# A four-block graph network on one core: SyncE's list of transfers written anew, and ScalarE's wait for its receivers' one-hots cut in two

## The reference

```
h = max(layernorm(x), 0); x = x + relu(mean_dst(h[src]) @ W_l.T + b_l + h @ W_r.T)              # L0
h = max(layernorm(x), 0); h1 = relu(mean_dst(h[src]) @ W1l + b1 + h @ W1r)                      # L1A
                          x = x + mean_dst(h1[src]) @ W2l + b2 + h1 @ W2r                       # L1B
h = max(layernorm(x), 0); x = x + LN(h + relu(h @ Ws.T + bs + mean_src(h[dst] @ Wn.T + bn)))    # L2
h = max(layernorm(x), 0); x = x + gcn(relu(gcn(h, W1, b1)), W2, b2)                             # L3A, L3B
```

## Time and profile before

| | before |
|---|---|
| median of 3 runs | 694.64 us (693.9 to 694.92) |
| the profiled execution | 693.28 us, span 691.5 us |
| mean granted clock of TensorE | 0.97 |
| TensorE busy | 631.2 us, 91% of the span |
| VectorE / ScalarE / GpSimd busy | 401.4 / 303.9 / 85.3 us |
| chain that ended last | TensorE 76%, DMA 8%, VectorE 6%, SyncE's queue 4%, issue 3% |

### The profile page before, as it was taken

The page is one execution under the profiler, slowest core; times in us unless marked ns, Lnnn a source line. Parts: engine busy times, 40 slices in busy tenths (PEclk is TensorE's granted clock), DMA queues, the critical chain, the costliest instruction groups (busy, mean ns, idle before and its releaser), DMA issues.

```text
span 691.5 us, 11104 instructions
## 1 busy us (share of the span) xinstructions
PE 631.2 (91%) x3047; PEld 512.7 (74%) x3048; DVE 401.4 (58%) x875; ACT 303.9 (44%) x628; POOL 85.3 (12%) x135
## 2 busy tenths in 40 slices
PE   6889999999108999999999896999999999999997
PEld 4556677778106888888888775888888898889886
DVE  6989989858108653333355476865599942350312
ACT  5968766642004345432123223222458864464320
POOL 4433432100000000000000000000135243000000
PEclk9999999999658999999999998999999999999999
DMA  6200425215785342124244424544210000000102
GB/s 226 84 1 21 55 41 76 40 62 95 142 196 139 68 95 64 61 68 120 56 95 97 100 78 102 138 95 101 63 61 2 0 2 1 0 1 1 46 16 90
DMA packets 151842, 48.38 MB, mean 70 GB/s; under 512 B 133500, under 2 KB 137396, under 8 KB 151800
## 3 DMA queue, kind: packets, MB, share of 16 engines
q1 hardware_dynamic: 150520, 45.34, 28.2%
q10 hardware_dynamic: 1280, 2.56, 1.0%
HBM read 30.44 MB, written 17.44 MB: 69 GB/s over the span
## 4 chain that ended last, share of the span: by engine, by line
PE 76%; DMA 8%; DVE 6%; SPq 4%; issue 3%; ACT 1%; POOL 0%; DVEq 0%; ACTq 0%; POOLq 0%
PE ps L1667 30%; PE ps L1760 18%; PE ps L1797 12%; PE ps L1823 8%; PE ps L1646 7%; DMA rows<-squares 2%; SPq L467 2%; SPq L449 2%; DMA wstage<-in_L_gnn_W1r 2%; DMA count_rows<-count_squares 2%; DMA swap<-count 1%; DVE src_hot L1159 1%; DVE stats L1131 1%; DVE own L1380 1%; DMA wstage<-rows 1%
## 5 line engine op out<-in xcount | busy, mean ns | idle before, releaser
L1760 PE MATMUL ps<-p_hi,cstage 128*128 128x512 f32 x400 | 158.8, 397 | 43.0 <-DVE own L1380 37.6
L1760 PE MATMUL ps<-p_lo,cstage 128*128 128x512 f32 x400 | 157.8, 394 | 0.0
L1667 PE MATMUL ps<-w_hi,hT_hi 128*128 128x512 f32 x320 | 126.2, 395 | 0.6 <-issue 0.4
L1667 PE MATMUL ps<-w_hi,hT_lo 128*128 128x512 f32 x320 | 124.6, 390 | 0.0
L1667 PE MATMUL ps<-w_lo,hT_hi 128*128 128x512 f32 x320 | 124.6, 389 | 0.0
L1760 PEld LDWEIGHTS ps<-p_hi,cstage 128*128 128x128 f32 x400 | 76.6, 191 | 61.7 <-DVE own L1380 39.5
L1760 PEld LDWEIGHTS ps<-p_lo,cstage 128*128 128x128 f32 x400 | 76.5, 191 | 15.9
L1646 PE MATMUL ps<-src_hot,dst_hot 128*128 128x320 bf16 x420 | 65.5, 300 | 7.4 <-DVE src_hot L1159 4.3
L1159 DVE TENSOR_SCALAR src_hot<-iota,nodeT 128x640 bf16<-128x640 f16 x210 | 68.6, 384 | 5.5 <-PE ps L1646 3.5
L1667 PEld LDWEIGHTS ps<-w_hi,hT_hi 128*128 128x128 f32 x320 | 60.1, 188 | 13.4 <-issue 0.9
L1667 PEld LDWEIGHTS ps<-w_hi,hT_lo 128*128 128x128 f32 x320 | 60.1, 188 | 12.6
(11 more groups left out here) (156 smaller groups left out, 963.3 us busy)
## 6 DMA issues: line engine op xcount, KB each, us to landing
rows<-squares SPq DMA_DIRECT2D x38, 256.0 KB, 2.4
zT<-rows SPq DMA_DIRECT2D x120, 64.0 KB, 2.5
count_rows<-count_squares SPq DMA_DIRECT2D x10, 320.0 KB, 2.2
countT<-count_rows SPq DMA_DIRECT2D x40, 80.0 KB, 3.2
x<-in_x ACTq DMA_DIRECT2D x1, 2304.0 KB
out_x<-x SPq DMA_DIRECT2D x9, 256.0 KB
wstage<-rows SPq DMA_DIRECT2D x32, 64.0 KB, 2.4
wstage<-in_L_gnn_W SPq DMA_DIRECT2D x2, 1024.0 KB, 5.6
```

The lines of the kernel that those rows point to most:

```text
L1667: last = nc.tensor.matmul(ps[:, bank, :], a[:, r, k, :], w[:, slot, k, :], start=n == 0, stop=n == len(pairs) - 1)
L1760: last = nc.tensor.matmul(ps[:, AGG + r, :], cstage[:, part, k, :], p_[:, k, :], start=n == 1, stop=n == 2 * len(parts) * NT)
```

## The change

1. SyncE's list. Parking and turning become steps of their own ("tp" and "tr" for counts, "park" and "turn" for the rest), so other steps stand between them. W1r is loaded behind the parking of count block 6, ahead of four turns of count blocks, bias row and swap, instead of behind them all. The swap moves from L0's aggregation to the products of L1B, behind the parking of tile 9. The turns of L2's weights are interleaved with those of L1B's tiles.
2. VectorE makes squares earlier (`SQUARED_AT`): all ten of L1B in L1A's aggregation, W_neigh's four pieces in the first four products of L1B, W_self's four at i = 1 and 2 of L1B's aggregation (were 2 and 3), six of L1A's and L2's tiles during the aggregation ahead (were four).
3. Turned weight pieces count on semaphores of their own (`weight_in`), turned counts on two (`cT_loaded[k]`), and a count turn from block 2 on waits until the turn two blocks back has landed.
4. ScalarE, in `receivers`, waits for the first half of its ring ahead of the first `apart` and for the second half ahead of the third, instead of for the whole ring ahead of the first.

Nothing is computed otherwise. A part on GpSimd's general path, which doesn't run here, is left out below.

```diff
+    SQUARED_AT = {L0: [(), (), (0,), (1,), (), (), (2,), (3,), (4,), (5,)], L1A: [(i,) for i in range(NT)],
+                  L1B: [(), (), (), (0,), (1,), (2,), (3,), (4,), (5,), ()]}
...
-            turns = {s: [("h", (s, i)) for i in range(NT)] for s in (L1A, L1B, L2)}
-            order += [("t", b) for b in range(BY_COUNTING)] + loads[:1] + [("t", b) for b in range(BY_COUNTING, NT)]
-            order += [("v", rows[2]), ("s", None)] + loads[1:2]
-            order += turns[L1A][:2] + loads[2:3] + [("v", rows[5])] + turns[L1A][2:]
-            order += loads[3:4] + turns[L1B][:2] + [("v", rows[6])] + loads[4:5] + turns[L1B][2:]
-            turned_weights = [("h", (None, j)) for j in range(2 * KF)]
-            order += turned_weights[:KF] + loads[5:6] + turned_weights[KF:] + turns[L2][:2] + loads[6:7] + turns[L2][2:]
+            def tail(s):
+                return [step for i in range(6, NT) for step in turns(s, i - 2) + parks(s, i)] + turns(s, 8, 9)
+
+            W = None
+            order += [step for b in range(BY_COUNTING) for step in (("tp", b), ("tr", b))] + loads[:1]
+            order += [("tp", 6)] + loads[1:2] + [("tr", 6), ("tp", 7), ("tr", 7), ("tp", 8)] + parks(L1A, 0)
+            order += [("tr", 8), ("tp", 9)] + parks(L1A, 1) + [("tr", 9)] + turns(L1A, 0, 1) + [("v", rows[2])]
+            order += loads[2:3] + [("v", rows[5])]
+            order += parks(L1A, 2) + turns(L1A, 2) + parks(L1A, 3) + turns(L1A, 3) + parks(L1A, 4, 5) + tail(L1A)
+            order += loads[3:4] + parks(L1B, 0, 1) + turns(L1B, 0, 1) + [("v", rows[6])] + parks(L1B, 2, 3, 4, 5)
+            order += loads[4:5] + turns(L1B, 2) + parks(L1B, 6) + turns(L1B, 3) + parks(L1B, 7, 8, 9) + [("s", None)]
+            order += turns(L1B, 4) + parks(W, 0) + turns(L1B, 5) + parks(W, 1) + turns(W, 0) + turns(L1B, 6) + parks(W, 2)
+            order += turns(W, 1) + turns(L1B, 7) + parks(W, 3) + turns(W, 2) + turns(L1B, 8) + turns(W, 3) + turns(L1B, 9)
+            order += loads[5:6] + parks(W, 4, 5) + turns(W, 4) + parks(W, 6) + turns(W, 5) + parks(W, 7) + turns(W, 6)
+            order += parks(L2, 0) + turns(W, 7) + parks(L2, 1) + turns(L2, 0, 1) + parks(L2, 2, 3) + loads[6:7]
+            order += turns(L2, 2) + parks(L2, 4) + turns(L2, 3) + parks(L2, 5) + tail(L2)
...
+                elif kind == "tr":
+
                     sp.wait_ge(counts_parked, 16 * (what + 2))
+                    if what > 1:
+                        sp.wait_ge(cT_loaded[what % 2], 64 * (what // 2))
...
                     if s is not None:
                         sp.wait_ge(lo_done, tile(s, i - 2))
+                    elif i > 1:
+                        wait_turned_weight(sp, i - 2)
...
                     t = tile_at(act, n, offset)
-                    act.wait_ge(first_rows[h], n + RING)
                     for e in range(BY_ACT):
+                        if e % 2 == 0:
+                            act.wait_ge(first_rows[h], n + (1 + e // 2) * RING // 2)
                         nc.scalar.activation(apart[h][:, e:e + 1, :], tab[:, window(b, h), :], ACT.Abs, scale=-1.0,
...
                             lo(s, i + 2, i % 2)
-                        if i < NT - 4:
-                            square(s, i + 4, i % 2)
-                        elif s == L1B:
-                            square_weight(i - (NT - 4))
+                        if i < 4:
+                            if s == L1B:
+                                square_weight(i)
+                            else:
+                                square(s, i + 6, i % 2)
...
-                        if s == L1B and i in (2, 3):
-                            square_weight(KF + 2 * i - 4)
-                            square_weight(KF + 2 * i - 3)
-                        if i in (2 + late, 3 + late):
-                            square(s + 1, i - 2 - late, i % 2)
-                        if i in (6, 7):
-                            square(s + 1, i - 4, i % 2)
+                        if s == L1B and i in (1, 2):
+                            square_weight(KF + 2 * i - 2)
+                            square_weight(KF + 2 * i - 1)
+                        for k in SQUARED_AT[s][i]:
+                            square(s + 1, k, k % 2)
```

More of the change, by code:

```diff
@@ L228, in gnn_kernel @@
     nodes_placed = sem("nodes_placed")
-    counts_ready, counts_out, cT_loaded = sem("counts_ready"), sem("counts_out"), sem("cT_loaded")
+    counts_ready, counts_out, cT_loaded = sem("counts_ready"), sem("counts_out"), [sem(f"cT_loaded{k}") for k in range(2)]
     vec_loaded = [sem(f"vec{k}_loaded") for k in range(5)]
@@ L250, in gnn_kernel @@
     normed, squared = sem("normed"), sem("squared")
-    parked, turned_in = [[sem(f"{what}{r}") for r in range(2)] for what in ("parked", "turned_in")]
+    parked, turned_in, weight_in = [[sem(f"{what}{r}") for r in range(2)] for what in ("parked", "turned_in", "weight_in")]
     counts_squared, counts_parked = sem("counts_squared"), sem("counts_parked")
@@ L286, in gnn_kernel @@
     BY_COUNTING = 6
+    SQUARED_AT = {L0: [(), (), (0,), (1,), (), (), (2,), (3,), (4,), (5,)], L1A: [(i,) for i in range(NT)],
+                  L1B: [(), (), (), (0,), (1,), (2,), (3,), (4,), (5,), ()]}
     def wait_turned_counts(engine, blocks=NT):
-        engine.wait_ge(cT_loaded, 64 * blocks)
+        for k in range(2):
+            if blocks > k:
+                engine.wait_ge(cT_loaded[k], 64 * ((blocks + 1 - k) // 2))
     def squares_of(dram, m):
@@ L298, in wait_parked, with wait_turned, wait_turned_weight @@
         engine.wait_ge(parked[(n - 1) % 2], 8 * (n + 1 - (n - 1) % 2))
-    def wait_turned(engine, n, r):
-        engine.wait_ge(turned_in[r], 32 * (n + 1 - r))
+    def wait_turned(engine, s, i, r):
+        engine.wait_ge(turned_in[r], 32 * (NT * (s - L1A) + i + 2 - r))
+    def wait_turned_weight(engine, j):
+        engine.wait_ge(weight_in[j % 2], 64 * (j // 2 + 1))
     def wait_loaded(engine, n):
@@ L439, in _, with parks, turns @@
-            turned_weights = [("h", (None, j)) for j in range(2 * KF)]
-            order += turned_weights[:KF] + loads[5:6] + turned_weights[KF:] + turns[L2][:2] + loads[6:7] + turns[L2][2:]
+            def parks(s, *tiles):
+                return [("park", (s, i)) for i in tiles]
+            def turns(s, *tiles):
+                return [("turn", (s, i)) for i in tiles]
+            def tail(s):
+                return [step for i in range(6, NT) for step in turns(s, i - 2) + parks(s, i)] + turns(s, 8, 9)
@@ L450, in _ @@
                             "p h (c q) d -> p (h c) (q d)", q=2).rearrange("p c (g i) -> p c g i", i=32),
-                            squares_of(count_rows[what], m)).then_inc(cT_loaded, 16)
-                elif kind == "h":
+                            squares_of(count_rows[what], m)).then_inc(cT_loaded[what % 2], 16)
+                elif kind == "park":
+                    s, i = what
+                    n = nth(s, i) if s is not None else nth_weight(i)
+                    sp.wait_ge(squared, n)
+                    sp.dma_start(rows_dram[n - 1], squares[:, (n - 1) % 2, :]).then_inc(parked[(n - 1) % 2], 16)
+                elif kind == "turn":
                     s, i = what
@@ L456, in _ @@
                     r = (n - 1) % 2
-                    sp.wait_ge(squared, n)
-                    sp.dma_start(rows_dram[n - 1], squares[:, r, :]).then_inc(parked[r], 16)
                     if n == 1:
@@ L467, in _ @@
                         sp.dma_start(to.rearrange("p k (g i) -> p k g i", i=32),
-                                     squares_of(rows_dram[n - 1], m)).then_inc(turned_in[r], 16)
+                                     squares_of(rows_dram[n - 1], m)).then_inc(
+                                         (turned_in if s is not None else weight_in)[r], 16)
                 elif kind == "s":
@@ L631, in _ @@
                     else:
-                        with pool.Fori(0, NT) as i:
+                        if s == L0:
+                            wait_turned_counts(pool, BY_COUNTING)
+                        with pool.Fori(0, BY_COUNTING) as i:
+                            general_columns(i)
+                        for i in range(BY_COUNTING, NT):
+                            if s == L0:
+                                wait_turned_counts(pool, i + 1)
                             general_columns(i)
```

8 lines of the change are left out of this document (3 added, 5 removed).

## The result

| | before | after |
|---|---|---|
| median | 694.43 us (693.9 to 694.92, 4 runs) | 656.77 us (656.55 to 658.13, 4 runs) |
| ratio of the two | | 0.9462, 95% interval 0.9445 to 0.9478 |
| profiled execution | 693.28, span 691.5 | 656.83, span 655.0 |
| mean granted clock | 0.97 | 0.997 |

A forecast was written before the change was run, and what follows sets the result against it. TensorE, busy 631.2 of 691.5 us, was taken as the bound, so only idle time and slow clock could be won. Terms -28.3 + 0.6 - 12.2 = -39.9 took 694.64 to 654.7 us, range 650 to 662.

The forecast's parts named there:

- What can be had back: Two losses of TensorE: L0's aggregation could end 36.1 us earlier undisturbed, and 12.2 us are lost in L1B's aggregation.
- Term 1, the load's data: Count blocks before L0's aggregation: W1r's early load pushes block 6's turn and block 7's parking back 2.8 us.
- Term 2: L0's aggregation: TensorE waits 4.2 us before tile 6, slow clock costs 2.4, and it ends 28.3 us earlier.
- Term 3, L1A: L1A's products and aggregation: nothing lost, 54.4 + 45.3 us, although VectorE comes 7 us late from L0.
- Term 4, the swap: L1B's products: the moved swap delays tile 4's turn, 0.6 us lost; behind it the margin falls to 2 us and holds.
- Rival B: L1B's products: the swap shows, TensorE waits over 5 us and the clock falls, giving 662.4 us; chance 0.14.
- Term 5, L1B's aggregation: L1B's aggregation: L2's weight pieces are turned earlier, so 12.2 us are won.
- Term 6, the ring: Counting: ScalarE waiting by halves of its ring wins at most 3.7 us, loses at most 1.6; taken as 0.
- A: Before L0's aggregation: W1r's early load costs nothing, giving 651.3 us; chance 0.16.
- C: L0's tail: each of four remaining steps lands 1 us later, 4 us in all, giving 658.7 us; chance 0.12.
- E: L0's aggregation: a wait holds W1r's load back until block 9 is turned, giving 664.5 us; chance 0.02.
- D: Whole kernel: slower than before by more than 0.2%, 1.4 us; chance 0.01.

The follow-up runs named there:

- later_in_tail: Against both_moved: in L0's aggregation W1r's split and L1A's first two hT tiles come later, W2l loads behind L1A's turns; 648.27 us, 0.9352 of the plain kernel before.
- start_base: The kernel before plus only an asserted bound on the loaded loop bounds of the counting; 698.88 us, 1.0045 of the plain kernel before.
- load_alone: Against start_base: W1r loaded right behind W1l, ahead of count block 6, swap left ahead of L1A's first turns; 691.36 us, 0.9926 of the plain kernel before.
- load_and_swap: Against load_alone: the swap also moved behind L1A's turns, ahead of W2r's load; 675.4 us, 0.9695 of the plain kernel before.
- load_first: Against the changed kernel with asserted loop bounds: W1r loaded right behind W1l, ahead of parking count block 6; 656.83 us, 0.9473 of the plain kernel before.
- swap_in_l1a: Against the changed kernel with asserted loop bounds: swap moved behind L1A's last turn, ahead of W2r's load; 655.51 us, 0.9433 of the plain kernel before.
- ring_undone: Against the changed kernel with asserted loop bounds: ScalarE waits for the whole ring ahead of its first receiver again; 659.99 us, 0.9506 of the plain kernel before.
- both_moved: load_first and swap_in_l1a together, on the changed kernel with asserted loop bounds; 653.77 us, 0.9428 of the plain kernel before.

## Why the prediction was right, and where it was off

The time, 656.77 us, is 2.1 over the forecast of 654.7 and inside 650 to 662. Part of that closeness is luck: the 39.9 us were read off the profiled execution, and the forecast starts from a median 1.36 us above it. Profiled execution against profiled execution it is 656.83 for 653.4, 3.4 us over. By its own steps:

1. *What can be had back.* Right: later_in_tail brings L0's aggregation to 46.07 us from start_base's 83.14, 37.1 us for the 36.1 read, and the 12.2 of L1B's aggregation are all won. load_alone and load_and_swap show that the 36.1 were held by more than the load: with it gone the swap held TensorE at tile 8, and with that gone 4.71 us at tile 8 were left, behind L1A's first turned tile.
2. *Term 1, the load's data.* Right in kind, off in form and size. It was to appear as a parking of 5.7 us; it appeared in the issuing of block 6, 5.00 instead of 3.46, and the parking took 3.4. load_first puts it at 1.4 us (stage) to 2.4 us (times) instead of 2.8. W1r itself took 6.4 us to land, not the 5.2 of the row that the term used.
3. *Term 2.* L0's aggregation was to be 28.3 us less from the start of the span; from its own start it is 28.1 less. The gap at tile 6 was forecast at 4.2 and measured at 4.07, tile 8 had a gap of 0.78 us where none was forecast. That the sum fits within 0.2 us is in part luck: measured from the aggregation's start, tile 5 started 0.7 us earlier than forecast (term 1 was too large), and tile 8's gap gave that back. The slow clock was charged at 2.4 us and took 2.3 (21.18 us for the last 80 matmuls, less the gap and 18.13).
4. *Term 3, L1A.* Right, no gap.
5. *Term 4, the swap.* The term that was mis-sized: 0.6 forecast, 2.6 measured. The way out took 9.5 us (304.30 to 313.82) as forecast. The way in and the turn behind it were to take 7.8 + 2.1; they took 11.0 (313.82 to 324.8), and the turn's four transfers needed 6.14 us to issue instead of 2.6. What came of it is a gap of 2.23 us, just over the sign of at most 2. Rival B named the mechanism, at more than twice its size. swap_in_l1a shows that the swap's place was the whole of it. The slow clock behind the gap adds 1.4 in some executions. And behind the swap the margin did not hold as forecast: a round of the queue was to take 5.8 us for each 5.44 of products, the rows show 6.1 to 6.4 (the turns of tiles 5 to 8 were issued at 323.46, 329.52, 335.92 and 342.24), and `hT_lo` of tiles 5 to 9 was ready 2.6, 1.6, 0.8, 0.2 and 0.15 us ahead of TensorE instead of 2. In ring_undone tile 9 came late, with a gap of 0.45 us.
6. *Term 5, L1B's aggregation.* Right to 0.1: 12.2 us. But no run tests its cause by itself. All kernels with the old list there take 57.5 to 59.8 us, also when the load and the swap are moved, and all with the new one 45.33; that the earlier turning of L2's weight pieces does it is read from the traces, and which part does it, the list or VectorE's earlier squares, is open.
7. *Term 6, the ring.* Right: nothing.

What is left of the difference is the counting, which ended 0.76 us later in the one profile, no more than it scatters among kernels with equal counting (149.47 in load_first, 151.81 in both_moved), and 0.4 us from L2 on; both are unexplained.

Of the other rivals, A (the load costs nothing) is out by load_first, C (a tail 4 us longer) by block 9's turn, which ended at 185.98 against a forecast 185.5 although the counting ended 0.76 us later, and E by W1r's issue at 159.24. D, a clock held down, didn't come either: in all fourteen traces, from L0's aggregation to L1B's, the clock was low for at most some 15 matmuls behind a gap.

## What to carry to other kernels

When one wait of TensorE is long, list everything that stands ahead of the released step in the in-order queue and in the in-order programs of the engines it passes: here a load, then the swap, then (by the traces) a turn held TensorE once the one ahead of it was gone, and freeing only the first brought 9 of 36 us. A transfer that used to lie in a stall has to be given a new cover of its own full length: the swap and the turn behind it took 20.5 us (304.30 to 324.80), and the queue had such a pause one layer earlier (240.9 to 261.6 in swap_in_l1a). Place work that nobody needs yet (a weight's split) behind the steps that the busy engine waits for; that last edit brought as much as moving the swap did.

## What the runs showed of the hardware

- A gap of TensorE of about 2.2 us (2.12 to 2.27) at the same place, tile 4 of L1B's products, was followed by half the clock in three of five kernels' profiled executions and by the full clock in two; where it fell, that stage took 1.4 us longer (58.36 against 57.01). In the fourteen traces together, from L0's aggregation to L1B's: behind all gaps of 2.98 us and more the clock fell, behind none of 1.87 us or less, and of the ten between 2.12 and 2.66 us behind six (2.13, 2.19, 2.27, 2.51, 2.65, 2.66) and not behind four (2.12, 2.23, 2.32, 2.55).
- Transfers behind a large one don't only land later, they are issued more slowly: 5.00 instead of 3.46 us for four count transfers behind 1 MB (changed kernel and load_first), 6.14 instead of 2.6 us for four of a turn behind the swap. SyncE's queue is held for that time.
- Assertions on loaded loop bounds, 20 with a register step each on every one of four engines, came with 3.1 and 3.2 us more of 695 and 657; by the profiles 1.8 and 1.6 us of that lie in the counting.
